# One attention and mixture-of-experts layer on one core: the expert inputs and x1 turned by transposing DMAs, with x1's rows kept as half-precision pairs

## The chip, the cores and the metric

The kernel runs on 1 core of one Trainium2 chip, in one launch. The metric is the device time of one execution, in microseconds (us). The runs of the kernel before have a median of 424.5 us (423.6 to 426.48, three runs).

## The reference

4 sequences of 1024 tokens with 128 channels go through one attention block and one mixture-of-experts block, each with a residual and a layer norm. Cut to what matters:

```python
q, k, v = silu(x @ Wq), silu(x @ Wk), x @ Wv          # 16 heads of 8
energy = einsum('bhnd,bhmd->bhnm', rope(q), rope(k)) * tril
out = einsum('bhnm,bhmd->bhnd', energy, v) * sigmoid(x @ Wg1 @ Wg2)
x1 = layernorm(x + (norm(out) * ln_w + ln_b) @ Wo)    # called x1 in the kernel
top_v, top_i = top_k(x1 @ gate_w, 2)                  # 8 experts, 2 for each token
g, u = x1 @ Wg[e], x1 @ Wu[e]                         # 128 -> 352
expert_out = sum over the 2 experts of p[e] * (silu(g) * u) @ Wd[e]
shared = (silu(x1 @ Sg) * (x1 @ Su)) @ Sd             # 176 wide, every token
y = layernorm(x1 + expert_out + shared)
```

The attention has no softmax, so the kernel computes it as a causal linear attention with a running state.

## The kernel before

The 4096 tokens are 32 tiles of 128 rows (P = 128), in 8 quads of 4 tiles (R = 4). The program for each engine is written out by hand, with semaphores between them; nothing is planned by a tool. It has four stages.

**Setup** (to 17 us) loads and splits weights.

**Attention, x1 and routing** (17 to about 196 us) run as one software pipeline: a loop over steps s = 0 to 37 on every engine, and in step s each engine works on the pieces of several tiles. Of tile t, the energies are made in step t, masked and summed in t+1, projected in t+2 (L583), and in t+3 ACT writes the normalised x1 twice (L796), as two rows of 132 f32 values in SBUF (`x1_rows`: 128 channels, the destination DEST, the gate weight). In step t+4 PE turns the row (L580, a transpose against the identity into the bank `b_p`), ACT copies the result to f16 (`x1T_hi`, L778), and DVE subtracts that from the PSUM value and so gets the low half (`x1T_lo`, L1000). In step t+5 PE multiplies both halves with the router's weights (L558 to L560). The order in a step on DVE is: masks, `x1T_lo`, routing work in some steps, `rope_add`, `add_x`, `x1_shifted`, `gate`, statistics, `rope_cos` (L920). The variance of x1 goes round four engines: ACT sums squares (L788), POOL makes `rstd` (L1280, L1282), DVE makes `x_plus` and `x_shift` (L970, L978), ACT writes x1 (L796). After each quad is ranked, POOL scatters its rows to DRAM with 8 indirect DMAs (L1288, 64 in all, each of 128 rows), one to the region of each token's first expert and one to that of its second. SP loads the inputs' transposed tiles (L416), one in each step.

**Shared expert and the end of routing** (about 180 to 237 us): the shared expert's matmuls over quads (L600 to L602, L616, L617) with DVE's `shared_add` (L1058), the table of slot tiles (DVE), and SP's 8 fill DMAs behind each expert's region.

**Routed experts** (237 to 391 us): 39 slot tiles of 256 slots, of which 35 hold real slots and the rest are dummies. They go through a ring of U = 4 buffers. For slot tile t: SP reads its address from a table (a value load), waits until PE has turned tile t-4 and DVE has copied its `slot_meta`, and loads 256 rows of 528 bytes (L442, from DRAM into `slot_rows`). PE turns them (L654, two f32 transposes into the bank `b_in`, in `slot_turn`). ACT copies the result to f16 (L861), DVE subtracts for the low half (L1174, in `evac`), and then copies DEST and WEIGHT out of the row (L1178); this last copy waits until the scatter of tile t-4 has landed (`y_scattered`). PE makes gate and up (L669 to L671, 18 matmuls of 256 columns, f16), ACT the silu (L869, three), DVE the product (L1186, three), PE the down projection in f32 (L685, 12 records, into the single bank `y_ps`), ACT the scaling by the gate weight (L880, two), and POOL scatters the result to `ydram` in DRAM (L1321, two indirect DMAs of 128 rows).

PE's order of work is fixed: up of tile t, turn of tile t+1, down of tile t-1. Up of t waits for DVE's low half of t (`slots_copied`); down of t-1 waits for `hidden_done` of t-1 and for the scaling of t-2, since there is one y bank.

**End** (to 425 us): SP reads four counts (`real_scatters`, L446), waits for the last scatters (L449), loads the results (L452, 16 DMAs of 256 KB), and PE, DVE and ACT make the last sum and layer norm, which SP stores (L460).

## Time and profile before

| | |
|---|---|
| runs, median (lowest to highest) | 424.5 us (423.6 to 426.48) |
| profiled execution, its own time | 426.87 us |
| its span in the profile | 425.0 us |
| mean granted TensorE clock | 0.959 of full |
| busy in the span: PE, PEld, DVE, ACT, POOL | 347.0, 271.8, 257.6, 235.0, 233.5 us |
| chain that ended last, by engine | PE 51%, DVE 15%, issue 11%, ACT 10% |

PE is the matmul engine and PEld its weight loads, which overlap it. The profiled execution is 1.9 us longer than its span, and 2.4 us longer than the median of the runs.

### The profile page before, as it was taken

How to read it: one execution, taken by the hardware profiler on the slowest of the kernel's cores; microseconds unless marked ns; L12 is line 12 of the kernel's file. 1: busy time of each engine (PE TensorE's matmuls, PEld its weight loads, DVE VectorE, ACT ScalarE, POOL GpSimd, SP SyncE). 2: the span in 40 equal slices, each digit the busy share in tenths (PEclk: the TensorE clock that was granted, in tenths of full speed). 3: DMA queues.
4: the chain of work that ended last, by engine and by line, in shares of the span. 5: the costliest groups of instructions: out<-in, count | busy, mean ns of one | idle time of the engine just before them, and what ended most of it. 6: DMA issues, size and time to landing. Idle time of an engine off the chain costs nothing.

```text
span 425.0 us, 12763 instructions
## 1 busy us (share of the span) xinstructions
PE 347.0 (82%) x4172; PEld 271.8 (64%) x4172; DVE 257.6 (61%) x826; ACT 235.0 (55%) x861; POOL 233.5 (55%) x302
## 2 busy tenths in 40 slices
PE   3798888787978887886489898897977979889980
PEld 2476656565756655645347797877977878779730
DVE  1469998978797879787555443333443433434682
ACT  3587779687877868523112354444454444445354
POOL 3377636768585868777640044534444345344682
PEclk9999999999899989999969999989999899899986
DMA  8956000101011110101232022212212222121784
GB/s 222 331 165 152 16 22 20 47 29 45 28 47 34 41 41 21 35 25 49 64 107 66 27 65 68 73 50 64 77 57 59 63 61 74 52 71 38 219 294 131
DMA packets 32280, 33.47 MB, mean 79 GB/s; under 512 B 4784, under 2 KB 27632, under 8 KB 32080
## 3 DMA queue, kind: packets, MB, share of 16 engines
q1 hardware_dynamic: 27360, 23.19, 18.9%
q0 software_dynamic: 4544, 9.45, 6.8%
q8 instruction: 36, 0.59, 0.6%
q14 instruction: 20, 0.16, 0.1%
q10 hardware_dynamic: 320, 0.08, 0.1%
HBM read 21.16 MB, written 13.56 MB: 82 GB/s over the span
## 4 chain that ended last, share of the span: by engine, by line
PE 51%; DVE 15%; issue 11%; ACT 10%; another core or an unknown queue 3%; POOL 3%; DMA 2%; SPq 2%; DVEq 1%; ACTq 0%; POOLq 0%
PE b_p L685 9%; PE b_es L671 6%; PE b_es L669 5%; PE b_es L670 4%; DVE masked_energies L938 4%; PE b_in L477 3%; PE b_es L502 3%; ACT turns L763 2%; PE b_es L514 2%; ACT ffn_staged L869 2%; PE b_o L534 2%; DMA x_rows<-ydram 2%; PE b_in L654 1%; PE b_o L528 1%
## 5 line engine op out<-in xcount | busy, mean ns | idle before, releaser
L1321 POOL DMA_INDIRECT ydram<-ffn_staged,slot_meta x78 | 74.9, 960 | 111.6 <-ACT ffn_staged L880 92.1
L1186 DVE TENSOR_TENSOR ffn_staged<-ffn_staged,b_es 128x256 f32<-128x256 f32 x79 | 31.8, 420 | 78.3 <-ACT ffn_staged L869 57.6
L1288 POOL DMA_INDIRECT rows<-x_rows,place x64 | 65.4, 1023 | 16.0 <-issue 13.6
L669 PE MATMUL b_es<-slots_T,w_hi 128*128 128x256 f16 x158 | 45.4, 287 | 19.2 <-DVE slots_T L1174 18.3
L685 PE MATMUL b_p<-w_down,ffn_staged 128*128 (+1 forms) x468 | 58.7, 275 | 1.0 <-issue 1.0
L685 PEld LDWEIGHTS b_p<-w_down,ffn_staged 128*128 128x128 f32 (+1 forms) x468 | 55.3, 191 | 1.2 <-issue 1.1
L869 ACT ACTIVATE ffn_staged<-b_es 128x256 f32<-128x256 f32 x79 | 29.2, 385 | 33.9 <-PE b_es L671 28.3
L763 ACT ACTIVATE turns<-b_turn,const_sb 128x128 f32<-128x128 f32 x128 | 36.5, 368 | 16.6 <-PE b_turn L488 15.9
L671 PE MATMUL b_es<-slots_T,w_lo 128*128 128x256 f16 x158 | 45.4, 287 | 0.0
L670 PE MATMUL b_es<-slots_T,w_hi 128*128 128x256 f16 x158 | 45.3, 287 | 0.0
L880 ACT ACTIVATE ffn_staged<-b_p,slot_meta 128x128 f32<-128x128 f32 x78 | 24.4, 366 | 35.9 <-PE b_p L685 34.1
L938 DVE TENSOR_TENSOR masked_energies<-b_es,const_sb 128x512 f32<-128x512 f32 x64 | 41.0, 680 | 1.8 <-PE b_es L502 1.4
L477 PE MATMUL b_in<-w_raw,xT_ring 128*128 128x384 f32 x64 | 30.6, 564 | 9.2 <-DMA ln_w_b<-in_ln 6.7
L796 ACT ACTIVATE x_rows<-x_plus,x_shift,rstd 128x256 f32<-128x256 f32 x32 | 19.2, 600 | 27.4 <-DVE x_shift L978 27.0
L1253 POOL TENSOR_TENSOR turned_qk<-qk,const_sb 128x256 f32<-128x256 f32 x32 | 26.2, 820 | 13.5 <-ACT qk L738 13.4
L669 PEld LDWEIGHTS b_es<-slots_T,w_hi 128*128 x158 | 16.0, 101 | 23.9 <-issue 21.3
L752 ACT ACTIVATE v_spread<-b_in 64x64 f32<-64x64 f32 x128 | 28.3, 221 | 1.1
L528 PEld LDWEIGHTS b_o<-turns,states 128*128 128x128 f32 x56 | 8.9, 196 | 30.9 <-DVE products L948 25.4
L1280 POOL TENSOR_TENSOR var_eps<-stat,const_sb 128x2 f32<-128x2 f32 x33 | 7.2, 219 | 36.4 <-ACT squares_out L788 36.1
L502 PE MATMUL b_es<-turns 32*64 32x128 f32 x1024 | 25.5, 286 | 1.7 <-issue 1.0
L920 DVE TENSOR_TENSOR roped<-qk,const_sb 128x256 f32<-128x256 f32 x32 | 23.0, 720 | 6.0 <-ACT qk L738 5.9
L528 PE MATMUL b_o<-turns,states 128*128 128x128 f32 x56 | 13.8, 330 | 15.2 <-DVE products L948 12.4
(213 smaller groups left out, 914.6 us busy)
## 6 DMA issues: line engine op xcount, KB each, us to landing
ffn_staged<-rows SPq DMA_DIRECT2D x39, 132.0 KB, 2.1
x_rows<-ydram SPq DMA_DIRECT2D x16, 256.0 KB, 6.8
xT_ring<-in_xT SPq DMA_DIRECT2D x32, 64.0 KB, 1.8
x_sb<-in_x SPq DMA_DIRECT2D x4, 512.0 KB, 6.1
out<-x_sb SPq DMA_DIRECT2D x8, 256.0 KB, 2.3
ffn_staged<-in_Wg SPq DMA_DIRECT2D x1, 1408.0 KB, 7.5
ffn_staged<-in_Wu SPq DMA_DIRECT2D x1, 1408.0 KB, 6.7
ydram<-ffn_staged,slot_meta POOLq DMA_INDIRECT x78
```

The lines of the kernel that those rows point to most:

```text
L477: nc.tensor.matmul(b_in[:, 0:3 * P], x_t, w_raw[:, :], start=True, stop=True).then_inc(projected, 1)
L502: mm = nc.tensor.matmul(b_es[H * h:H * h + H, g, P * c:P * c + P], keys[g], queries[g][:, 2 * h:2 * h + 2, H * c:H * c + H], start=True, s ...
L669: nc.tensor.matmul(o, w, slots_T[:, j % 2, 0, :], start=True, stop=False)
L670: nc.tensor.matmul(o, w, slots_T[:, j % 2, 1, :], start=False, stop=False)
L671: mm = nc.tensor.matmul(o, wlo, slots_T[:, j % 2, 0, :], start=False, stop=True)
L685: mm = nc.tensor.matmul(y_ps[:, b * P:(b + 1) * P], hidden_T[0:n, k % 2, c, b * P:(b + 1) * P], w_down_flat[0:n, bass.ds(e * (IC * P) + c ...
L763: nc.scalar.activation(turns[:, t % TR, j * P:(j + 1) * P], b_turn[:, P:2 * P], ACT.Copy, scale=C("spread")[:, j:j + 1])
L869: nc.scalar.activation(silu_gate[:, j % 2, c, :], up_banks[j % 2][c][:, 0:SLOTS], ACT.Silu).then_inc(expert_silu_done[c], 1)
L938: nc.vector.tensor_tensor(masked_energies[:, t % 2, 2 * r:2 * r + 2, :].rearrange("p c (b n) -> p c b n", n=H), b_es[:, 2 * r:2 * r + 2, 0 ...
L1186: ins = nc.vector.tensor_tensor(hidden_T[:, j % 2, c, :], silu_gate[:, j % 2, c, :], up_banks[j % 2][c][:, SLOTS:], ALU.mult)
L1288: nc.gpsimd.indirect_dma_start(out=rows, out_offset=bass.IndirectOffsetOnAxis(ap=place[:, t // R, c, t % R:t % R + 1], axis=0), in_=x1_row ...
L1321: nc.gpsimd.indirect_dma_start(out=ydram, out_offset=bass.IndirectOffsetOnAxis(ap=slot_meta[:, j, b, 0:1].bitcast(u32), axis=0), in_=scale ...
```

## The change

It does the following.
- A row of `x1_rows` holds x1 as 128 f16 high halves and 128 f16 low halves, in the 512 bytes where 128 f32 values stood; the f32 x1 stays in `x_sb`. ACT writes `x_sb` and the high halves in two instructions of 128x128 in place of one of 128x256; DVE makes the low halves (`rows_lo`) at the end of its step, after `rope_cos`.
- PE's transpose of x1, ACT's `x1T_hi` and DVE's `x1T_lo` are gone. SP issues a transposing DMA for each tile, SBUF to SBUF (`turn_x1`), in its loop of input loads; after every fourth tile a plain DMA copies copy 0 of the quad's rows to copy 1. POOL's scatters wait for `x1_lo_done`, and the second copy's for `rows_doubled`.
- For a slot tile, SP issues a transposing DMA from DRAM straight into `slots_T` (now 4 buffers), then waits until the scatter of tile t-4 has landed, and issues a small DMA for `slot_meta` (256 pieces of 8 bytes); the load of the next tile stands behind both. PE's `slot_turn`, ACT's `slots_hi` and DVE's `evac` are gone.
- Up of t waits for its load and for `hidden_done` of t-2. There are two y banks, and down of t-1 waits for the scaling of t-3.

```diff
 x1_rows = sb("x1_rows", [P, TILES, TOP, ROW])
+x1_halves = x1_rows[:, :, :, :].bitcast(f16)
...
 projected_out = b_p[:, 0:2 * P]
-x1T_ps = b_p[:, 2 * P:3 * P]
...
 shared_y = [b_turn[:, :], b_o[:, :]]
-slots_T_ps = b_in[:, 0:SLOTS]
-y_ps = b_p[:, 0:SLOTS]
+y_ps = [b_p[:, 0:SLOTS], b_in[:, 0:SLOTS]]
...
                 sp.dma_start(w_down_chunks[0:n, :, c, :], Wd[:, c * P:c * P + n, :].rearrange("e i h -> i e h")).then_inc(ffn_loaded, 16)
+    def turn_x1(t):
+        if not tile(t):
+            return
+        sp.wait_ge(x1_lo_done, t + 1)
+        sp.dma_start_transpose(x1T[:, :, t * P:(t + 1) * P], x1_halves[:, t, 0, 0:2 * P]).then_inc(x1T_loaded[t % R], 16)
+        if t % R == R - 1:
+            quad = x1_halves[:, t + 1 - R:t + 1, :, 0:2 * P]
+            sp.dma_start(quad[:, :, 1, :], quad[:, :, 0, :]).then_inc(rows_doubled[t // R % 2], 16)
...
             load_ffn(t // 2 - XR // 2)
+        turn_x1(t - 7)
+    for t in range(TILES - 7, TILES):
+        turn_x1(t)
...
         if exists(t - U):
-            sp.wait_ge(slots_turned, t - U + 1)
-            sp.wait_ge(meta_copied, t - U + 1)
+            sp.wait_ge(expert_up_done[IC - 1], t - U + 1)
             sp.wait_ge(table_loaded, 16)
-        sp.dma_start(slot_rows[:, j, :, :], rows[bass.ds(at, SLOTS), :].rearrange("(p b) w -> p b w", p=P)).then_inc(slots_loaded[j], 16)
+        sp.dma_start_transpose(slots_T[:, j, :, :], row_halves[bass.ds(at, SLOTS), 0:2 * P]).then_inc(slots_loaded[j], 16)
+        if exists(t - U):
+            sp.wait_ge(y_scattered[j], 32 * i)
+            sp.wait_ge(table_loaded, 16)
+        sp.dma_start(slot_meta[:, j, :, :], rows[bass.ds(at, SLOTS), DEST:DEST + 2].rearrange("(b p) w -> p b w", p=P)).then_inc(meta_loaded[j], 16)
...
             t = s - 5
+            pe.wait_ge(x1T_loaded[t % R], 16 * (t // R + 1))
...
                 last = nc.tensor.matmul(ends_ps, all_ones, first_places, start=False, stop=True)
-        if tile(s - 4):
-            pe.wait_ge(x1_done, s - 3)
-            last = nc.tensor.transpose(x1T_ps, x1_rows[:, s - 4, 0, 0:P], C("identity"))
...
             pe.wait_ge(masked[0], TILES); pe.wait_ge(masked[1], TILES); pe.wait_ge(products_masked, TILES)
-        pe.wait_ge(x1T_lo_done, R * q + R); pe.wait_ge(x1T_hi_done, R * q + R)
+        for k in range(R):
+            pe.wait_ge(x1T_loaded[k], 16 * (q + 1))
...
             shared_up(q + 2)
-    def slot_turn(i, j, lag):
-        ok, t, k, r = stage(i, j, lag)
-        if not ok:
-            return
-        pe.wait_ge(slots_loaded[k], 16 * (r + 1))
-        if exists(t - 1):
-            pe.wait_ge(slots_copied, t)
-        for b in range(2):
-            mm = nc.tensor.transpose(slots_T_ps[:, b * P:(b + 1) * P], slot_rows[:, k, b, 0:P], C("identity"))
-        mm.then_inc(slots_turned, 1)
...
         t = U * i + j
-        pe.wait_ge(slots_copied, t + 1)
+        pe.wait_ge(slots_loaded[j], 16 * (i + 1))
+        if exists(t - 2):
+            pe.wait_ge(hidden_done, t - 1)
...
                 w, wlo = w_hi_flat[:, bass.ds(at, P)], w_lo_flat[:, bass.ds(at, P)]
-                nc.tensor.matmul(o, w, slots_T[:, j % 2, 0, :], start=True, stop=False)
-                nc.tensor.matmul(o, w, slots_T[:, j % 2, 1, :], start=False, stop=False)
-                mm = nc.tensor.matmul(o, wlo, slots_T[:, j % 2, 0, :], start=False, stop=True)
+                nc.tensor.matmul(o, w, slots_T[:, j, 0, :], start=True, stop=False)
+                nc.tensor.matmul(o, w, slots_T[:, j, 1, :], start=False, stop=False)
+                mm = nc.tensor.matmul(o, wlo, slots_T[:, j, 0, :], start=False, stop=True)
...
         pe.wait_ge(hidden_done, t + 1)
-        if exists(t - 1):
-            pe.wait_ge(yscaled[(j + lag - 1) % U], i + (j + lag - 1) // U + 1)
+        if exists(t - 2):
+            pe.wait_ge(yscaled[(j + lag - 2) % U], i + (j + lag - 2) // U + 1)
...
                 n = min(P, INNER - c * P)
-                mm = nc.tensor.matmul(y_ps[:, b * P:(b + 1) * P], hidden_T[0:n, k % 2, c, b * P:(b + 1) * P],
+                mm = nc.tensor.matmul(y_ps[k % 2][:, b * P:(b + 1) * P], hidden_T[0:n, k % 2, c, b * P:(b + 1) * P],
...
     pe.wait_ge(v_done, TILES)
-    slot_turn(0, 0, 0)
...
         return a[:, FT * q:FT * q + FT, :].rearrange("p t c -> p (t c)")
-    pe.wait_ge(slots_copied, SLOT_TILES)
+    pe.wait_ge(hidden_done, SLOT_TILES)
+    pe.wait_ge(yscaled[(SLOT_TILES - 2) % U], (SLOT_TILES - 2) // U + 1)
...
         nc.scalar.activation(gate_tanh[:, t % GR, :], gate_ps, ACT.Tanh, scale=0.5).then_inc(gate_tanh_done, 1)
-    def x1T_hi(t):
-        if not tile(t):
-            return
-        nc.scalar.activation(x1T[:, 0, t * P:(t + 1) * P], x1T_ps, ACT.Copy).then_inc(x1T_hi_done, 1)
...
         act.wait_ge(x1_shift_done, t + 1)
-        both = x_plus[:, t % 2, :].unsqueeze(1).broadcast_to([P, TOP, P])
-        nc.scalar.activation(x1_rows[:, t, :, 0:P], both, ACT.Identity, scale=rstd[:, 1 - t % 2, 1:2], bias=x1_shift[:, t % 2:t % 2 + 1]).then_inc(x1_done, 1)
+        for to in (x_sb[:, t, :], x1_halves[:, t, 0, 0:P]):
+            ins = nc.scalar.activation(to, x_plus[:, t % 2, :], ACT.Identity, scale=rstd[:, 1 - t % 2, 1:2], bias=x1_shift[:, t % 2:t % 2 + 1])
+        ins.then_inc(x1_done, 1)
...
     for s in range(LAST_STEP + 1):
-        if tile(s - 2) or tile(s - 4):
+        if tile(s - 2):
...
         squares(s - 2)
-        x1T_hi(s - 4)
...
         shared(q)
-    def slots_hi(i, j, lag):
-        ok, t, k, r = stage(i, j, lag)
-        if not ok:
-            return
-        act.wait_ge(slots_turned, t + 1)
-        nc.scalar.activation(slots_T[:, k % 2, 0, :], slots_T_ps, ACT.Copy).then_inc(slots_hi_done, 1)
...
         nc.vector.bn_aggr(stat[:, 1 - t % 2, 1:3], moment_parts[:, t % 2, :]).then_inc(x1_moments, 1)
-    def x1T_lo(t):
-        if not tile(t):
-            return
-        dve.wait_ge(x1T_hi_done, t + 1)
-        nc.vector.tensor_tensor(x1T[:, 1, t * P:(t + 1) * P], x1T_ps, x1T[:, 0, t * P:(t + 1) * P], ALU.subtract).then_inc(x1T_lo_done, 1)
+    def rows_lo(t):
+        if not tile(t):
+            return
+        dve.wait_ge(x1_done, t + 1)
+        nc.vector.tensor_tensor(x1_halves[:, t, 0, P:2 * P], x_sb[:, t, :], x1_halves[:, t, 0, 0:P], ALU.subtract).then_inc(x1_lo_done, 1)
...
         dve.wait_ge(shared_y_done, q + 1); dve.wait_ge(x1_done, R * q + R)
-        nc.vector.tensor_tensor(x_sb[:, R * q:R * q + R, :], shared_y[q % 2].rearrange("p (t c) -> p t c", t=R), x1_rows[:, R * q:R * q + R, 0, 0:P],
+        nc.vector.tensor_tensor(x_sb[:, R * q:R * q + R, :], shared_y[q % 2].rearrange("p (t c) -> p t c", t=R), x_sb[:, R * q:R * q + R, :],
...
             split_lo(s - TILES)
-        if s >= 5:
-            dve.wait_ge(x1T_hi_done, min(s - 3, TILES)); dve.wait_ge(squares_summed, min(s - 1, TILES))
-        x1T_lo(s - 4)
+        if quad_ranked(s) is not None or quad_routed(s) is not None or quad_second(s) is not None:
+            dve.wait_ge(squares_summed, min(s - 1, TILES))
...
         rope_cos(s + 3)
+        rows_lo(s - 3)
...
             split_lo(q + 4)
-    def evac(i, j, lag):
-        ok, t, k, r = stage(i, j, lag)
-        if not ok:
-            return
-        dve.wait_ge(slots_hi_done, t + 1)
-        nc.vector.tensor_tensor(slots_T[:, k % 2, 1, :], slots_T_ps, slots_T[:, k % 2, 0, :], ALU.subtract).then_inc(slots_copied, 1)
-        if exists(t - U):
-            dve.wait_ge(y_scattered[k], 32 * r)
-            dve.wait_ge(yscaled[k], r)
-        nc.vector.tensor_copy(slot_meta[:, k, :, :].bitcast(i32), slot_rows[:, k, :, DEST:DEST + 2].bitcast(i32)).then_inc(meta_copied, 1)
...
     def scatter(t, c):
+        if t % R == 0 and c == 1:
+            pool.wait_ge(rows_doubled[t // R % 2], 16 * (t // R // 2 + 1))
...
             pool.wait_ge(placed, t // R + 1); pool.wait_ge(weighed, t // R + 1); pool.wait_ge(destinations_set, 1)
+            pool.wait_ge(x1_lo_done, t + R)
```

## Rows read from the trace of the kernel before

**Rows 1.** Windows: start:end, length, then busy us (instructions) of PE, PEld, DVE, ACT, POOL, clock, DMA share, GB/s.
```profile
17.00:180.00 163.00, 138.68 (x2573) 102.19 (x2580) 136.32 (x428) 124.76 (x533) 113.61 (x165) 0.98 0.19 56
180.00:237.29 57.29, 43.89 (x334) 28.65 (x314) 37.18 (x111) 14.20 (x35) 28.27 (x31) 0.94 0.21 60
237.29:388.06 150.77, 132.40 (x1142) 120.72 (x1143) 59.37 (x180) 70.11 (x212) 65.09 (x68) 0.97 0.22 61
...
277.40:280.80 3.40, 3.40 (x19) 2.43 (x17) 0.84 (x2) 0.77 (x2) 1.92 (x2) 0.51 0.28 78
```

**Rows 2.** Chain in order of time, one slot tile: start us, us, what.
```profile
256.83 1.76 another core or an unknown queue
...
259.37 0.39 ACT ffn_staged L869
```

**Rows 3.** Waits, 237 to 388: engine line, waited for, us in total, times, longest.
```profile
PE b_es L669 <- DVE slots_T L1174: 18.3, 9, 2.5
```

**Rows 4.** Timeline, two slot tiles: start us, us, engine line, operation [idle before].
```profile
302.65 0.27 PE L669 MATMUL b_es<-slots_T,w_hi 128*128 128x256 f16 x1
...
304.61 0.38 PE L654 MATMUL b_in<-const_sb,ffn_staged 128*128 128x128 f32 x2
...
304.83 1.50 PE L685 MATMUL b_p<-w_down,ffn_staged 128*128 x12
...
306.17 0.27 PE L669 MATMUL b_es<-slots_T,w_hi 128*128 128x256 f16 x1
...
306.45 0.63 ACT L880 ACTIVATE ffn_staged<-b_p,slot_meta 128x128 f32<-128x128 f32 x2 [0.98 <-PE b_p L685]
...
307.83 0.96 POOL L1321 DMA_INDIRECT ydram<-ffn_staged,slot_meta  x1 [0.75 <-issue]
...
309.10 0.96 POOL L1321 DMA_INDIRECT ydram<-ffn_staged,slot_meta  x1 [0.30 <-issue]
```

**Rows 5.** DMA queues, 310.6 to 311.0: queue, packets, MB, share.
```profile
q0 software_dynamic: 32, 0.07, 53.1%
```

**Rows 6.** SP's first four slot loads in the timeline; landing of all 39.
```profile
226.31 3.67 SPq L442 DMA_DIRECT2D ffn_staged<-rows  x4
...
DMA to landing us min/median/max: 2.0/2.1/2.9
```

**Rows 7.** Groups by line, whole span: operation xcount, busy us, mean ns, idle before.
```profile
L796 ACT ACTIVATE x_rows<-x_plus,x_shift,rstd 128x256 f32<-128x256 f32 x32 | 19.2, 600 | 27.4 <-DVE x_shift L978 27.0
L778 ACT ACTIVATE x1T<-b_p 128x128 f16<-128x128 f32 x32 | 9.3, 291 | 0.4 <-PE b_p L580 0.4
L1000 DVE TENSOR_TENSOR x1T<-b_p,x1T 128x128 f16<-128x128 f32 x32 | 9.1, 285 | 11.4 <-ACT x1T L778 10.5 <-ACT squares_out L788 0.5
L920 DVE TENSOR_TENSOR roped<-qk,const_sb 128x256 f32<-128x256 f32 x32 | 23.0, 720 | 6.0 <-ACT qk L738 5.9
```

**Rows 8.** Timeline, attention: DVE near the end of a step, PE's logits.
```profile
134.07 0.54 DVE L920 TENSOR_TENSOR roped<-qk,const_sb 128x256 f32<-128x256 f32 x1
...
139.12 0.17 PE L558 MATMUL b_p<-router_w_hi,x1T 128*128 128x8 f16 x1
```

**Rows 9.** Timeline, the last tile's x1 and its logits.
```profile
195.28 0.60 ACT L796 ACTIVATE x_rows<-x_plus,x_shift,rstd 128x256 f32<-128x256 f32 x1 [2.22 <-DVE x_shift L978]
...
198.69 0.17 PE L558 MATMUL b_p<-router_w_hi,x1T 128*128 128x8 f16 x1
```

**Rows 10.** Chain in order of time, the last real scatter.
```profile
391.20 0.95 POOL ydram L1321
...
394.26 0.79 DMA ydram<-ffn_staged,slot_meta
```

**Rows 11.** SP's value loads of line 446: count, ns min/median/max, first and last start.
```profile
L446 SPq TENSOR_LOAD <-real_scatters x4: 18/270/303, 381.2 to 383.3; - x4
```

**Rows 12.** Page, DMA issues: operation xcount, KB each, median us to landing.
```profile
x_rows<-ydram SPq DMA_DIRECT2D x16, 256.0 KB, 6.8
...
xT_ring<-in_xT SPq DMA_DIRECT2D x32, 64.0 KB, 1.8
```

## What the change does to the time

> **What bounds the kernel now.** I read the windows by stage first [rows 1]. In the experts' stage PE is busy 132.40 of 150.77 us and no other engine over half, so PE is near its limit there; in the attention stage PE (138.68 of 163.00) and DVE (136.32) share the work. Then the chain of waits, in order of time, for what PE waits on in the experts' stage. In one slot tile of four ACT waits in the middle of its silus for something that the profile can't name, 1.76 us at 256.83, and its last silu ends only at 259.76 [rows 2]. What PE waits for is then DVE's low half of the next tile: 18.3 us in 9 waits, about 2.0 each, the longest 2.5 [rows 3]. Eight of the nine are such late events, one for each pass of the ring of four. They hold up silu, and because ACT's and DVE's halves of the next tile stand behind silu and product in program order, they reach PE. In undisturbed tiles PE runs without a gap: up 302.65 to 304.61 (1.96 us), turn 0.22, down 1.34, next up at 306.17 [rows 4], so 3.52 us a tile.
>
> **The change part by part, experts.** Between 237.29 and 388.06 lie 36 ups and 35 downs.
> PE loses 36 turns of 0.22: −7.9 us. The turned halves no longer depend on ACT and DVE, so a late silu doesn't stop the next up; PE can do down of t-1 and up of t+1 before it needs the late product, 3.3 us of cover for a delay of about 2.0. The 18.3 us go, if nothing else is late. The bare sum of PE is 36 × 1.96 + 35 × 1.34 = 117.5, which is 33.3 less than now; 7.9 + 18.3 of it are named, and the rest is mostly the granted clock: in 277.40 to 280.80 it was 0.51 of full [rows 1], the lower of its two levels, 1.2 GHz, some us after PE had stood idle behind a late event, and the mean of 0.97 over the stage means 4.5 us lost. I keep a good half of it as clock loss that stays, 2.5.
>
> **What is late next.** ACT and DVE lose work and are busy 70.11 and 59.37 us even now [rows 1], so they are no bound. The new loop goes through DRAM: SP now waits for the scatter of tile t-4 between the transposing load of t and the load of t+1. From up of t to up of t+5: up, down, up, down on PE 6.60; scaling until 307.08, 0.91 after the down's end at 306.17; POOL begins 0.75 later and its second scatter 1.27 after the first (307.83, 309.10) [rows 4]. That scatter's packets run at 310.6 to 311.0, so it lands about 1.9 to 2.2 us after its start [rows 5]; the last real one of the stage took until 395.05, 3.85 after 391.20 [rows 10], and I take 2.2 with 3.85 as the upper end. On SP follow the small DMA's issue and the next value load, together the spacing of SP's loads, (3.67 − 0.34)/3 = 1.11 [rows 6]. Then L, the time of the transposing DMA. The sum is 12.84 + L for 5 tiles.
> No row shows a transposing DMA. Its lower bound is the plain load of the same rows, 2.0 to 2.1 [rows 6]; the nearest upper row is the DMA of 256 KB at 6.8, one of 16 in flight together [rows 12]. I take 3.0, near the plain load, because size and direction are the same and one is in flight at a time. With L = 3.0 a tile takes 15.8/5 = 3.17, just under PE's 3.30: slack 16.5 − 15.84 = 0.66 in five tiles. A late event holds up the scaling of the tile before, which stands behind the silus in ACT's order, by about 1.4 (its 2.0 less some 0.6 of the 0.98 that ACT stands idle before a scaling [rows 4]). The slack takes 0.66 of it, so each of 8 events costs 0.74: 5.9. The stage comes to 117.5 + 5.9 + 2.5 + 0.5 for the first and last tiles = 126.4, **−24.4 us**.
> The Trainium skill ("VectorE: DVE Perf Modes", section "The three transpose paths") speaks against the change: a 128×128 two-byte transpose takes 390 ns on TensorE and 1309 ns by the DMA crossbar. For the four blocks of a slot tile that estimate gives 5.2 us, a tile of 3.6 us, and a sum about 11 us worse. Another page ("Advanced Engine Details and Errata", section "X-Bar Transpose (TRN2)") has transposing DMAs as fast as regular ones, which gives 2.1 and a sum about 4 us better.
>
> **Attention and routing, 17 to 180.** PE loses the turn (0.11 a step). ACT loses 0.29 a step [rows 7] (`x1T_hi`), and its one write of 0.600 becomes two of 128x128; the nearest rows are twice 0.29 (`x1T_hi`) and 0.60 for both halves together, so 0.57 to 0.74, taken 0.60: it ends no later. DVE's low half, 0.285, goes from the middle of the step to its tail, after `rope_cos` [rows 7]; it stays 0.285 if left alone, and may be longer beside POOL's work, as L920 is (0.54 at 134.07, 0.72 on average) [rows 7, 8]. In the tail it delays the next step's masks. The variance's loop over ACT, POOL and DVE spans two steps, so half of it counts: +0.15 in some 12 steps without routing work; in the routing steps the wait in the middle gets shorter, −0.13 in 14. The doubling DMA (256 KB a quad) and 32 more transfers may slow SBUF accesses: +0.1 a step, bounds −0.1 and +0.35. Sum **+3**, −4 to +12. A step is 163/32 = 5.1 us.
> SP's queue: after `x1_lo_done` of a step come the transposing DMA, then the next input load, needed two steps on in the same place of PE. From 134.07 + 0.54 + 0.28 for the low half and 0.1 for the semaphore, to the logits at 139.12, are 4.1 us [rows 8]. The transposing DMA is hidden up to L = 4.1; the input load behind it (0.34 issue, 1.8 landing [rows 6, 12]) has room too. Cover gone, each us of L costs half a us in 32 steps, 16 us. POOL's waits for the low halves and the doubled rows end long before: a quad's ranks come several steps after its x1.
>
> **180 to 237.** The last tile's x1 is written at 195.88; with low half, 0.1 twice and L = 3.0 its logits begin at 199.5, against 198.69 [rows 9]. **+1**, −1 to +4.
>
> **End.** SP's four value loads (L446) ran at 381.2 to 383.3, hidden [rows 11]. They now stand behind the last tiles' `slot_meta`, which waits for tile 34's scatter. That last one lands at 395.05, and only then come 0.34 and four value loads of 0.77 less what lies in the last, 2.9: **+3.3**, 0 to +4.5.
>
> **Sum.** −24.4 + 3 + 1 + 3.3 = −17.1. The profiled execution took 426.87, so 409.8; it stood 2.4 above the median of the runs, so the median comes to 424.5 − 17.1 = **407 us**.
>
> **Rivals.**
> (A) *PE alone bounds the experts*: L near 2.1 and scatters that land in 1.9 absorb the late events. For it: the loop has 1.7 us of slack then. Against: some landings are 3.85. −33.3 + 3 + 1 + 3.3 = −26: 398 us.
> (B) *The stalls come back in the new loop*: the late scaling delays the scatter, SP and the load, by as much as before. Only the turns are gained: −7.9 + 7.3 = −0.6: 424 us. For it: the loop has only 0.66 us to give.
> (C) *Slower: the transposing DMA sets the step.* Place: PE's wait for `x1T_loaded` ahead of the logits. Price: 16 × (L − 4.1) in attention; in the experts 7.2 us for each us of L (36/5), which gives 7.2 L − 49.9 with late events and clock; L − 2 more in 180 to 237; with +3 and +3.3 the total is about 24.2 L − 111. It decides from L = 4.6: 434 us at L = 5, 458 at L = 6. For it: no row shows such a DMA, and it may well be issued as several instructions of 0.34 each on SP, so that it doesn't do in one piece what the line says. Against: the plain rows of 64 and 132 KB are at 1.8 and 2.1.
>
> **Chances.** Forecast 0.47 (its own range 400 to 417), A 0.13, B 0.17, C 0.23. Changes under 1% (4.2 us) can't be told from none. Faster by over 1%: forecast and A, 0.60; within 1%: B, 0.17; slower: C, 0.23. The range takes in A with attention at its lower bound, about 393, and at the other end B and the beginning of C, 430; outside lie most of C and little of A.
>
> **What would show it.** Experts: no PE matmul of L654, PE's waits before up near zero, a tile of 3.3 to 3.4 us, the stage near 126. SP's transposing DMA: landing 3 (right), over 4.6 (C). Attention: 163 + 3, with PE's wait ahead of the logits no longer than now; in C that wait appears in every step. End: four value loads after the last scatter's landing, the first result load about 3 us behind it. The forecast is wrong if the transposing DMA lands after 4.6 us, if SP's or the DMA queue's order adds a wait that I counted at nothing, or if DVE's tail costs more than half of 0.285 a step.

## The result, and the profile after

The changed kernel takes 430.83 us (median of 20 runs, 425.22 to 437.86) against 424.5 us for the kernel before (20 runs, 420.17 to 433.64). The ratio is 1.0134, 95% interval 1.0103 to 1.0166: 1.3% slower, where 407 us was predicted. Some executions of each kernel are slower, at a lower granted clock, and all ratios here leave them out; that keeps 13 of these 20, but of the kernel before only 2 of 13 on the chip of f1_wdown, f3_pace, f4_best and f5_bestpace, whose ratios are therefore the least sure, and f3_pace's trace is of a slow execution. The profiled execution took 429.0 us, its span 427.1.

The head of the page of the changed kernel, and its windows, cut where the first and the last up of the experts begin (columns as in [rows 1]):

```profile
span 427.1 us, 12492 instructions
...
PE 343.0 (80%) x4062; PEld 261.5 (61%) x4062; DVE 243.1 (57%) x748; ACT 223.5 (52%) x822; POOL 234.6 (55%) x302
```

```profile
17.00:180.00 163.00, 130.82 (x2352) 95.90 (x2355) 131.79 (x398) 122.59 (x509) 106.20 (x155) 0.95 0.28 75
180.00:249.00 69.00, 53.75 (x515) 35.10 (x503) 44.80 (x134) 19.86 (x57) 35.41 (x41) 0.93 0.25 65
249.00:393.20 144.20, 133.04 (x1129) 116.71 (x1130) 43.77 (x112) 58.43 (x185) 69.11 (x72) 0.99 0.31 66
393.20:427.10 33.90, 17.61 (x67) 9.54 (x66) 18.14 (x88) 14.18 (x39) 17.76 (x22) 0.83 0.62 200
```

Fewer instructions, less work on PE, DVE and ACT, and a longer span. PE did 2352 matmuls by 180 us, where it had done 2573 before [rows 1]; the turns that are gone are only some 30 of the difference, so it is behind. The marks of the two kernels (start of the event in each trace, us):

| mark | before | after | difference of the stage |
|---|---|---|---|
| start of ACT's last write of x1 | 195.3 | 206.6 | +11.3 |
| last logits | 198.7 | 210.8 | +0.8 |
| first up of the experts | 237.3 | 249.0 | −0.4 |
| last up (39 tiles) | 395.0 | 393.2 | −13.5 |
| first result load | 395.1 | 396.0 | +2.7 |
| end of the span | 425.0 | 427.1 | +1.2 |

They add up to +2.1. The experts' stage did get shorter (4.15 us from up to up before, 3.79 after), by little more than half of what was predicted; the attention steps ate most of it, and the end took 4 us more.

**Attention.** Groups by line of the changed kernel between 60 and 180 us (operation xcount | busy us, mean ns | idle before), and under them the same `x_shift` instruction in the kernel before, between 60 and 170 us:

```profile
L789 ACT ACTIVATE x_sb<-x_plus,x_shift,rstd 128x128 f32<-128x128 f32 x21 | 10.4, 493 | 18.3 <-DVE x_shift L960 18.1
L789 ACT ACTIVATE x_rows<-x_plus,x_shift,rstd 128x128 f16<-128x128 f32 x21 | 10.0, 478 | 0.0
L982 DVE TENSOR_TENSOR x_rows<-x_sb,x_rows 128x128 f16<-128x128 f32 x21 | 8.6, 412 | 0.2 <-ACT x_rows L789 0.2
L960 DVE SCALAR_TENSOR_TENSOR x_shift<-stat,rstd 128x1 f32<-128x1 f32 x20 | 8.1, 406 | 0.0
```

```profile
L978 DVE SCALAR_TENSOR_TENSOR x_shift<-stat,rstd 128x1 f32<-128x1 f32 x20 | 3.0, 149 | 0.0
```

DVE's new low half takes 0.41 us on average: in 16 of the 21 steps 0.28 to 0.29, in five 0.81. `x_shift`, one column, went from 0.15 to 0.41 on average. The timeline of one step shows why (changed kernel; start us, us, engine, line):

```profile
127.29 0.34 DVE L952 SCALAR_TENSOR_TENSOR x_plus<-b_p,rstd,x_sb 128x128 f32<-128x128 f32 x1
127.34 0.47 POOL L1235 TENSOR_TENSOR states<-states,products 128x128 f32<-128x128 f32 x1
127.55 0.96 DVE L960 SCALAR_TENSOR_TENSOR x_shift<-stat,rstd 128x1 f32<-128x1 f32 x1
127.75 0.73 POOL L1221 TENSOR_TENSOR turned_qk<-qk,const_sb 128x256 f32<-128x256 f32 x1
128.43 0.28 DVE L940 SCALAR_TENSOR_TENSOR gated_out<-gate_tanh,b_o 128x128 f32<-128x128 f32 x1
```

`x_shift` ends at 128.51, when POOL's `turned_qk` ends (128.48). It was not late in starting; it stood in DVE beside POOL's work on SBUF. It is so each time: of the 20 in this window 13 took 0.15 us, and the other seven (0.42 to 1.22 us) all end 0.02 to 0.03 us after a `turned_qk`. The Trainium skill ("Trainium Architecture — The Big Picture", section "What this means for kernel authors") says that DVE and GpSimd share one pair of SBUF ports and that it is an exclusive lock; the rows agree. In the kernel before, other instructions met POOL (L920 took 0.72 on average, [rows 7]), and no `x_shift` did. Moving one instruction changed which. It also took some away: the routing's `gap` instruction (six of them between the eleventh and the last tile's x_plus) took 0.58 us before and 0.2 us or so now.

The transposing DMA of x1 was not slow. Its 32 instructions and their landing, and the one exception, in the chain of waits between 36 and 50 us (start us, us, what):

```profile
L416 SPq DMA_TRANSPOSE x1T<-x_rows x32: 1169/1177/3365, 32.7 to 207.9; - x32
...
DMA to landing us min/median/max: 2.3/2.3/7.1
```

```profile
36.94 0.29 DVE x_rows L982
37.24 7.12 DMA x1T<-x_rows
```

A median of 2.3 us, where 4.1 were free. Only the second one, issued right behind SP's three loads of w_down, took 7.1. On SP's queue the issue itself takes 1.18 us, not 0.34.

**Experts.** Waits of the changed kernel over its span (engine line waited for: us in total, times, longest):

```profile
ACT ffn_staged L854 <- remote: 40.4, 20, 3.4
...
PEld b_es L669 <- issue: 13.2, 24, 2.0
...
PE b_es L669 <- DMA slots_T<-rows: 6.1, 10, 1.8
```

"remote" is what the profile says where it sees no releaser. In the kernel before, the same row had 14.1 us in 14 waits. ACT's waits in the middle of its silus have tripled in time; they now come in 14 of the 39 tiles, where they came in 8, and where they are densest in every other one. One of them in the timeline:

```profile
278.66 0.96 POOL L1292 DMA_INDIRECT ydram<-ffn_staged,slot_meta  x1 [2.65 <-ACT ffn_staged L865]
...
279.92 0.96 POOL L1292 DMA_INDIRECT ydram<-ffn_staged,slot_meta  x1 [0.30 <-issue]
...
280.72 0.38 ACT L854 ACTIVATE ffn_staged<-b_es 128x256 f32<-128x256 f32 x1 [0.32 <-PE b_es L671]
281.19 0.96 POOL L1292 DMA_INDIRECT ydram<-ffn_staged,slot_meta  x1 [0.30 <-issue]
282.46 0.96 POOL L1292 DMA_INDIRECT ydram<-ffn_staged,slot_meta  x1 [0.30 <-issue]
284.45 0.38 ACT L854 ACTIVATE ffn_staged<-b_turn 128x256 f32<-128x256 f32 x1 [3.35 <-remote]
284.73 0.38 ACT L854 ACTIVATE ffn_staged<-b_o 128x256 f32<-128x256 f32 x1
```

PE had issued the last matmul of that up at 281.72 and gone on to the down, but the count that the second silu waits for arrived only at 284.42, and two more behind it, three within 0.3 us. Meanwhile POOL issued four scatters back to back. Before the change the scatters came in pairs with some 2.3 us between, and only one pair in four stood close behind another.

**End.** SP, in the chain of waits: the last small DMA, the last value load, the first result load.

```profile
392.99 0.39 SPq L455
...
395.36 0.27 SPq L459
...
396.05 0.35 SPq L465
```

### The profile page after: what moved, and what is told of

Same layout as the page of the kernel before. It is cut to its first block, busy times and chain, and to the rows that moved or that the text cites. A ratio compares the mean times of both kernels' runs of the same rounds, so it can differ in the third digit from the quotient of the medians.

```text
span 427.1 us, 12492 instructions
## 1 busy us (share of the span) xinstructions
PE 343.0 (80%) x4062; PEld 261.5 (61%) x4062; DVE 243.1 (57%) x748; ACT 223.5 (52%) x822; POOL 234.6 (55%) x302
## 4 chain that ended last, share of the span: by engine, by line
PE 35%; issue 17%; DVE 17%; SPq 10%; DMA 8%; ACT 7%; another core or an unknown queue 3%; POOL 2%; DVEq 0%; ACTq 0%; POOLq 0%
DVE masked_energies L920 4%; SPq L451 4%; PE b_es L515 3%; PE b_es L527 3%; PE b_o L547 3%; PE b_in L685 3%; DMA slots_T<-rows 2%; ACT turns L762 2%; DVE roped L902 2%; PE b_in L490 2%; DMA x_rows<-ydram 2%; SPq L446 2%; DMA x1T<-x_rows 2%; SPq L455 2%
## 5 line engine op out<-in xcount | busy, mean ns | idle before, releaser
L669 PE MATMUL b_es<-slots_T,w_hi 128*128 128x256 f16 x158 | 43.9, 278 | 8.6 <-DMA slots_T<-rows 6.1
L762 ACT ACTIVATE turns<-b_turn,const_sb 128x128 f32<-128x128 f32 x128 | 36.6, 368 | 17.1 <-PE b_turn L501 16.7
L670 PE MATMUL b_es<-slots_T,w_hi 128*128 128x256 f16 x158 | 43.6, 276 | 0.4 <-issue 0.4
L671 PE MATMUL b_es<-slots_T,w_lo 128*128 128x256 f16 x158 | 43.8, 277 | 0.0
L920 DVE TENSOR_TENSOR masked_energies<-b_es,const_sb 128x512 f32<-128x512 f32 x64 | 41.2, 681 | 1.7 <-PE b_es L515 1.0
L854 ACT ACTIVATE ffn_staged<-b_es 128x256 f32<-128x256 f32 x79 | 27.0, 397 | 18.0 <-PE b_es L671 13.5
L541 PE MATMUL b_o<-turns,states 128*128 128x128 f32 x56 | 13.5, 324 | 25.3 <-DVE products L930 25.3
L1221 POOL TENSOR_TENSOR turned_qk<-qk,const_sb 128x256 f32<-128x256 f32 x32 | 25.8, 805 | 12.2 <-ACT qk L737 12.1
L685 PE MATMUL b_in<-w_down,ffn_staged 128*128 (+1 forms) x228 | 30.0, 281 | 3.1 <-DVE ffn_staged L1156 3.0
L515 PE MATMUL b_es<-turns 32*64 32x128 f32 x1024 | 29.5, 300 | 3.6 <-issue 3.5
L789 ACT ACTIVATE x_sb<-x_plus,x_shift,rstd 128x128 f32<-128x128 f32 x32 | 15.8, 493 | 31.0 <-DVE x_shift L960 30.6
L685 PEld LDWEIGHTS b_in<-w_down,ffn_staged 128*128 128x128 f32 (+1 forms) x228 | 27.4, 193 | 6.2 <-issue 6.1
L685 PE MATMUL b_p<-w_down,ffn_staged 128*128 (+1 forms) x240 | 30.2, 275 | 0.0
L685 PEld LDWEIGHTS b_p<-w_down,ffn_staged 128*128 128x128 f32 (+1 forms) x240 | 28.4, 191 | 0.3
L1156 DVE TENSOR_TENSOR ffn_staged<-ffn_staged,b_turn 128x256 f32<-128x256 f32 x19 | 8.0, 421 | 34.6 <-ACT ffn_staged L854 20.6
```

The costliest lines, as they stand in the source:

```text
L515: mm = nc.tensor.matmul(b_es[H * h:H * h + H, g, P * c:P * c + P], keys[g], queries[g][:, 2 * h:2 * h + 2, H * c:H * c + H], start=True, s ...
L669: nc.tensor.matmul(o, w, slots_T[:, j, 0, :], start=True, stop=False)
L670: nc.tensor.matmul(o, w, slots_T[:, j, 1, :], start=False, stop=False)
L671: mm = nc.tensor.matmul(o, wlo, slots_T[:, j, 0, :], start=False, stop=True)
L685: mm = nc.tensor.matmul(y_ps[k % 2][:, b * P:(b + 1) * P], hidden_T[0:n, k % 2, c, b * P:(b + 1) * P], w_down_flat[0:n, bass.ds(e * (IC * ...
L762: nc.scalar.activation(turns[:, t % TR, j * P:(j + 1) * P], b_turn[:, P:2 * P], ACT.Copy, scale=C("spread")[:, j:j + 1])
```

## The experiments

A ratio is to the kernel before on the same chip, with its 95% interval; the chips differ, so marks from the traces are used beside it. "Ups" is the mean time from up to up over 39 tiles.

| kernel | ratio | last x1 at | first up | ups | ACT's "remote" waits in silus | span |
|---|---|---|---|---|---|---|
| before | 1 | 195.3 | 237.3 | 4.15 | 14.1 | 425.0 |
| changed | 1.013 (1.010 to 1.017) | 206.6 | 249.0 | 3.79 | 40.4 | 427.1 |
| e1_meta | 0.997 (0.993 to 1.000) | 209.4 | 250.7 | 3.80 | 44.7 | 425.1 |
| e2_space | 1.063 (1.056 to 1.071) | 207.2 | 249.4 | 4.36 | 0 | 453.6 |
| e3_lopool | 0.984 (0.976 to 0.991) | 199.6 | 241.6 | 3.78 | 53.5 | 419.2 |
| e4_ffn | 1.017 (1.007 to 1.026) | 210.0 | 256.5 | 3.83 | 43.7 | 436.1 |
| f1_wdown | 1.024 (1.013 to 1.034) | 207.7 | 249.8 | 3.79 | 34.8 | 426.6 |
| f3_pace | 1.011 (0.998 to 1.024) | 209.5 | 254.7 | 3.70 | 30.0 | 432.4 |
| f4_best | 0.975 (0.966 to 0.984) | 192.9 | 236.0 | 3.69 | 36.3 | 407.0 |
| f5_bestpace | 0.988 (0.978 to 0.999) | 194.8 | 236.5 | 3.67 | 18.2 | 411.8 |
| g1_x1pe | 1.002 (0.997 to 1.007) | 211.1 | 252.9 | 3.84 | 41.9 | 432.0 |
| g3_best_x1pe | 0.978 (0.969 to 0.987) | 197.6 | 239.0 | 3.79 | 49.4 | 413.4 |
| g2_metaspace | run once | 207.9 | 249.1 | 3.85 | 1.8 | 439.3 |
| h1_half | run once | 205.8 | 251.7 | 3.28 | 0 | 404.3 |

Kernels with the same attention code (changed, e1, e2, f3, g2; h1 adds eight DMAs to it) have their last x1 at 205.8 to 209.5: differences under 4 us in that column say nothing. Much of this spread is the granted clock. Between the eleventh and the last tile's x_plus (x_plus is what DVE makes just before ACT writes x1; 21 tiles) the windows are, in this order for the kernel before, the changed one, e3_lopool and f5_bestpace:

```profile
75.66:190.45 114.79, 95.26 (x1674) 68.08 (x1655) 95.33 (x314) 81.23 (x335) 85.89 (x120) 0.97 0.12 36
80.13:201.74 121.61, 95.83 (x1653) 68.12 (x1652) 99.69 (x315) 83.81 (x335) 83.68 (x120) 0.97 0.21 56
81.36:194.67 113.31, 89.09 (x1652) 63.47 (x1632) 90.87 (x293) 84.31 (x335) 94.81 (x141) 1.00 0.23 61
75.00:189.90 114.90, 90.86 (x1631) 65.83 (x1631) 90.67 (x293) 84.42 (x336) 94.18 (x141) 0.97 0.25 68
```

The changed kernel's steps are 6.8 us longer than those of the kernel before at the same clock, 0.97 of full. The same code has 121.7 in h1 (0.97), 122.5 in g2 (0.97), 124.2 in e1 (0.95), 123.2 in e2 (0.92) and 125.5 in f3 (0.89). So the clock can hide or feign some 4 us here, but it does not explain the slower steps. Nor does it explain the 11.3 us up to the last x1: h1, whose clock from 17 us to there is 0.98 as in the kernel before (the changed kernel has 0.96), is still 10.5 us behind it.

**e1_meta: the wait for the scatter off SP's queue.**
```diff
-                    sp.wait_ge(y_scattered[j], 32 * i)
+                    sp.wait_ge(meta_copied, t - U + 1)
-                sp.dma_start(slot_meta[:, j, :, :], ...
+                sp.dma_start(meta_in[:, j, :, :], ...
+                dve.wait_ge(y_scattered[k], 32 * r)      # in copy_meta, after hidden of the tile before
+                nc.vector.tensor_copy(slot_meta[:, k, ...], meta_in[:, k, ...]).then_inc(meta_copied, 1)
```


> From the changed kernel; SP no longer waits for the scatter of tile t-4 between two slot loads: the small DMA goes to a buffer of its own, and DVE copies it into slot_meta after the hidden product of the tile before, waiting there for the scatter. Theory: the loop scatter, SP, small DMA, value load, transposing load is what keeps the experts at 3.79 us a tile (145 us from the first to the last up), so the ups come about 3.45 us apart, the stage is 10 to 13 us shorter, and the four value loads before the results are hidden again (2 to 3 us). Whole kernel 10 to 14 us less than the changed one. Rival: the late counts of PE's progress that ACT waits for (3 us in every other tile) set the pace whatever SP does; then under 3 us.

The ups stay at 3.80: the loop through the scatter did not set the pace. The gain is at the end: the first result load comes 2.4 us before the last up, in the changed kernel 2.9 us after it, and from the last up to the end of the span are 30.0 us in place of 34.0. By the ratios the kernel is some 7 us faster than the changed one, between theory and rival; the traces show only these 4 of them, and a last x1 that is 2.8 us later.

**e2_space and g2_metaspace: scatters spaced by their landing.**
```diff
+                if spaced:
+                    pool.wait_ge(y_scattered[(j - 1) % U], 32 * (n if j else n - 1))
```


> From the changed kernel; POOL waits before each tile's two result scatters until those of the tile before have landed (its loop is written out for that). Theory that PE's counts come late because four scatters run back to back: the late counts (ACT waiting 2 to 3.4 us in the middle of a silu, 39 us in all) go, though each pair starts up to 1 us later; the stage is 0 to 8 us shorter. Rival: the bunches of four are only the consequence of late counts that have another cause; then the waits stay at about 39 us and the stage is 0 to 5 us longer.

> e1_meta with the full spacing of e2_space (POOL waits until both scatters of the tile before have landed). It tells whether e2_space was slow because of SP's loop through the scatter or because of POOL. Theory: POOL alone makes a tile 1.27 + 2.3 + 0.75 = 4.3 us, so the ups stay 4.2 to 4.4 apart even with the loads off that loop, and ACT has no waits of unknown cause in its silus. Rival: ups 3.4 to 3.7 apart.

In both, ACT's waits of unknown cause in the silus are gone, but for one of 1.8 us in g2. That answers the question of cause, but both are slow. In e2_space the later scatters hold up SP, and PE waits for the slots:

```profile
POOL ydram L1294 <- DMA ydram<-ffn_staged,slot_meta: 38.8, 16, 3.6
PE b_es L669 <- DMA slots_T<-rows: 33.6, 30, 2.5
```

With the loads off that loop (g2_metaspace) the ups are 3.85 apart, not the 4.3 that I expected of POOL alone; there DVE's copy waits for the scatters instead (32.2 us in 14 waits). Of the 12.2 us that g2's span is longer than the changed kernel's, 2.2 are in the experts' stage and 8.0 behind the first result load, where the granted clock was 0.70 of full and not 0.82.

**f3_pace and f5_bestpace: weaker spacing.** POOL waits for the first scatter of the tile before only.
```diff
+                if paced:
+                    pool.wait_ge(y_first[(j - 1) % U], 16 * (n if j else n - 1))
```


> From e1_meta; POOL waits before a tile's two result scatters until the first scatter of the tile before has landed (each half has its own semaphore, the loop is written out). Theory: four scatters back to back make PE's counts late, and since in e1_meta the scatters are off the path of the loads, spacing them costs little: ACT's waits in the middle of a silu fall from 44.7 us to under 10, ups come 3.4 to 3.6 us apart in place of 3.79, and it is 6 to 12 us faster than e1_meta. Rival: POOL itself becomes the bound, at 1.27 + landing 2.1 to 2.5 + 0.75 less the first scatter's own overlap, 3.0 to 4.2 us a tile; then no faster.

> f4_best with the spacing of f3_pace. The difference to f4_best is that of f3_pace to e1_meta: 6 to 12 us less if late counts from back-to-back scatters bound the experts, none or more if POOL becomes the bound.

The waits in the silus fall by a third (f3 against e1) to a half (f5 against f4), but in f5 another 19.4 us of them stand ahead of the scalings (7.4 in f3). The ups come closer by 0.1 (f3 against e1) and 0.02 (f5 against f4), and neither kernel is faster than the one that it was made from. A miss: this spacing does not stop the late counts and costs as much as it gives.

**h1_half: one scatter for each tile.** The second 128 slots of each tile are left out of the result.
```diff
-                for b in range(2):
+                for b in range(1):
                     nc.gpsimd.indirect_dma_start(out=ydram, ...
```


> e1_meta with one result scatter for each slot tile in place of two (the second 128 slots of each tile are left out of the result; ydram is filled beforehand with copies of x by eight DMAs in the attention steps, and the waits are counted accordingly). Only the experts' stage is to be read. Theory that POOL's back-to-back scatters make PE's counts late and that these cost the stage its last 0.3 to 0.5 us a tile: ACT's waits of unknown cause in its silus fall from 44.7 us to under 5, and the ups come 3.30 to 3.40 us apart, PE's own 1.96 + 1.34, in place of 3.79. Rival: the late counts have another cause; then the waits stay over 20 us and the ups over 3.5 apart.

The ups are 3.28 apart, and PE is busy all the time. The window of the stage, and two silu sequences with a scatter in each (timeline):

```profile
251.70:376.20 124.50, 124.49 (x1129) 116.31 (x1130) 51.06 (x152) 65.45 (x186) 34.46 (x36) 1.00 0.32 61
```

```profile
301.63 0.38 ACT L860 ACTIVATE ffn_staged<-b_turn 128x256 f32<-128x256 f32 x1 [0.27 <-PE b_turn L677]
301.70 0.96 POOL L1313 DMA_INDIRECT ydram<-ffn_staged,slot_meta  x1 [2.20 <-ACT ffn_staged L871]
302.29 0.38 ACT L860 ACTIVATE ffn_staged<-b_o 128x256 f32<-128x256 f32 x1 [0.27 <-PE b_o L677]
```

So the bare PE time of the prediction is right, SP's transposing loads keep up with it (PE has no wait for them here), and all that stands between 3.28 and 3.80 goes away when POOL issues half as many scatters. It halves the number, the time and the data of the scatters at once, so it doesn't say which of these holds the counts back, nor how much of the 0.52 us a tile goes through the late counts: in g2, where they are nearly gone too, the ups are 3.85 apart.

**e3_lopool: the low halves on POOL.**
```diff
-                rows_lo(s - 3)        # DVE, end of step
+                rows_lo(s - 4)        # POOL, ahead of powers(s)
```


> From the changed kernel; the low halves of x1 are made by POOL one step later, before the variance's power, in place of DVE at the end of its step; SP's transposing DMA is issued one input load later. Theory that DVE sets the attention steps: DVE loses 0.41 us a step, and the last x1 is written 6 to 10 us earlier than 206.6. Rival: the variance's loop or the DMAs set it; then POOL's extra 0.4 us ahead of the power makes it 0 to 6 us longer.

The last x1 comes 7.0 us earlier, as the theory has it (some of it with the clock, as said above), although here PE does wait for the transposing DMA:

```profile
L416 SPq DMA_TRANSPOSE x1T<-x_rows x32: 1167/1178/1929, 36.4 to 201.0; - x32
...
  PE b_p L570: 14.9, 11
```

**f1_wdown and e4_ffn: the big loads.** f1 issues SP's three w_down loads at tiles 14, 18 and 22; e4 issues all expert weights from ACT's queue.
```diff
-                if part == 2:
-                    for c in range(IC):
+                if part in (5, 7, 9):
+                    c = (part - 5) // 2
```


> From the changed kernel; SP's three loads of w_down, which stood just ahead of the second transposing DMA of x1, are issued one at a time at the input loads of tiles 14, 18 and 22, with a semaphore of their own. Theory: that transposing DMA took 7.1 us from issue to landing because those loads were ahead of it, and this is the lag that the changed kernel has from its fifth tile on; it now takes under 4 us and the whole kernel 3 to 5 us less than the changed one. Rival: the loads only delay another transposing DMA, wherever they stand; then under 1.5 us.

> From the changed kernel; the loads of the expert weights (two of 1408 KB and the rest) are issued by ACT into its own queue in steps 0, 2 and 4 in place of SP between its input loads. Theory: the 4.6 us that the changed kernel falls behind between 40 and 47 us come from the transposing DMAs and input loads standing behind those big loads in SP's queue; 3 to 5 us of them come back, less about 1 us of ACT's issue time. Rival: the 16 DMA engines themselves are full then, whatever the queue; then under 1 us.

In f1 every transposing DMA lands in 2.3 us:

```profile
DMA to landing us min/median/max: 2.3/2.3/2.3
```

But the kernel is no faster: 1.4 us ahead of the changed one at the eleventh tile's x_plus (78.7), where e2, f3 and h1, which keep these loads, have 79.1 to 79.2, and level at the last x1 (207.7 against 206.6). Nor is e4. Its first up comes 7.5 us later than the changed kernel's: it is 3.4 behind at the last x1 and loses 4.8 more between the last logits and the first up, where the clock was 0.84 of full and not 0.91 (f3 and h1 have 0.84 there too, and lose 3.4 and 4.1). The one long DMA was real, and was not worth 3 to 5 us. It may matter with e3's edit: e3_lopool has its fifth x_plus at 52.7 us, 5.3 later than the changed kernel, and f4_best, with both edits, at 45.1. Why e3 starts so late was not tested.

**g1_x1pe: x1 turned by PE again, the rows stay pairs.**
```diff
+                    last = nc.tensor.transpose(x1T_ps, x_sb[:, s - 4, :], C("identity"))
+                x1T_hi(s - 4)         # ACT
+                x1T_lo(s - 4)         # DVE, mid step
-                sp.dma_start_transpose(x1T[...], x1_halves[:, t, 0, 0:2 * P])
```


> From the changed kernel; the turn of x1 goes back to PE, ACT and DVE as in the kernel before (from the f32 x1), while the rows stay pairs: DVE still makes the low halves of the rows at the end of its step, ACT still writes x1 twice, the slots are still turned by DMA. Theory: the pairs are what costs in the attention steps and the transposing DMA is hidden, so undoing the DMA gives nothing back and adds ACT 0.29 and DVE 0.29 us a step: last x1 written 3 to 8 us later than 206.6 in the changed kernel. Rival: the transposing DMAs and the order of SP's queue cost the 11 us; then the last x1 is back within 4 us of the kernel before (195.3).

The last x1 comes 4.5 us later than in the changed kernel (1.6 to 5.3 against all those with its attention code), not earlier. The transposing DMA of x1 costs nothing and seems a small gain; the pairs are the cost.

**f4_best and g3_best_x1pe.** f4_best joins e1, e3 and f1; g3 is the same with the turn of x1 on PE.

> The meta buffer of e1_meta, the low halves on POOL of e3_lopool and the later w_down loads of f1_wdown together. If the three gains are independent (1.7, 2.9 and 1% of the changed kernel), 0.955 to 0.965 of the kernel before; if the lag of e3_lopool at its fifth tile (5.4 us behind the changed kernel) has the cause of f1_wdown's, up to 2% more.

> f4_best with the turn of x1 on PE, ACT and DVE as in g1_x1pe; the low halves of the rows stay on POOL. The difference to f4_best is the worth of the transposing DMA of x1 by itself: theory, f4_best is 3 to 8 us faster (ACT 0.29, DVE 0.29, PE 0.11 us a step, half or less of it on the path); rival, no difference, since the variance's loop over ACT, POOL and DVE sets the step.

f4_best is 2.5% faster than the kernel before by the ratio, somewhat less than was expected of the sum; the spans of the two traces, 407.0 against 425.0, are 4.2% apart. Its last x1 comes 13.7 us earlier than in the changed kernel; g3's comes 4.7 us after f4's, and 2.8 after that of f5, which has f4's attention code. The whole times of f4 and g3 can't be told apart (their intervals overlap, on different chips).

Between the eleventh and the last tile's x_plus, where the start plays no part, the steps alone give (us, from the traces; in brackets the granted clock): before 114.8 (0.97), changed 121.6 (0.97), g1 128.6 (0.95), e3 113.3 (1.00), f4 113.6 (0.98), f5 114.9 (0.97), g3 115.9 (0.97). Low halves on DVE rather than POOL: 8.3 (changed against e3), but 6.7 at the same clock (against f5). With the turn on PE in both, the same move is worth 12.7 (g1 against g3), of which some 2.6 may be the clock (e1 against the changed kernel). PE's turn rather than the DMA: on a DVE that is full 7.1 (g1 against changed) or, at g1's clock, 4.5 (against e1); on one that is not 1.0 to 2.3 (g3 against f5 and f4), which is within what two traces of the same code differ by.

## Why the prediction was wrong

**Bound now, bare PE sum: right.** The prediction has 3.30 a tile; h1_half has 3.28. **The time L of the transposing DMA: right**, 2.3 us for x1 in the trace, where 3.0 was taken, and no wait of PE for slots in h1_half. Rival C, which had this DMA set the step, did not happen: slower came by another way, the one I had written as "if DVE's tail costs more than half of 0.285 a step": the steps got 0.32 longer (6.8 us in 21). That the chances had 0.23 for slower is no merit, since it stood there for C.

**The step that failed first: attention, +3 predicted, +11.3 measured (range −4 to +12).** Two terms were mis-sized. The low half was to "stay 0.285"; it took 0.41 on average, since it now reads SBUF and in five of 21 steps meets POOL. And I counted only the instruction that moved: `x_shift` grew by 0.26 us because the order shifted it onto POOL's work, which no term held. The two add 0.38 us to a step, where I had none more and half of 0.285 moved. That is not all net: routing instructions that now miss POOL give some 0.15 back, and by the windows above DVE is busy 4.4 us longer in 21 steps (0.21 a step) and idle 2.5 us longer (0.12). The idle time is the rest of the miss: the emptier middle of the step gave nothing back, since DVE now waits there for the variance's power (8.3 us between 60 and 180, 0.9 before between 60 and 170). e3 and f5 show the size: DVE loses 8.8 to 9.0 us of work in 21 steps, and the steps get 8.3 (e3, at full clock) or 6.7 us (f5, at the clock of the changed kernel) shorter. So DVE's work counts by three quarters or more, and not by half. Of the 11.3 us, 6.8 fall in these 21 steps; the other 4.5 are there by the eleventh tile, at a like rate for each tile, and no experiment took them apart. ACT's two writes took 0.97 and not 0.60, a term that was also wrong; f5, which keeps them, has steps as long as the kernel before at the same clock (114.9 against 114.8), so they cost little.

The +3 itself was made of the wrong thing. The two terms of the low half cancelled (12 × 0.15 against 14 × 0.13), and all that was left, 32 × 0.1, was a slower SBUF under more DMA traffic. No run isolates that term, but h1_half speaks against it: with DMAs busy 0.31 of the time in these 21 steps against 0.21 its steps take 121.7 us against 121.6, at the same clock.

**Then the experts, the larger miss: −24.4 predicted for 36 ups and 35 downs, −13.5 measured over the stage.** The step that failed is "the 18.3 us go", with 8 events at 0.74 left of them. The turns' part came, 38 × 0.22 = 8.4; some 3 us are clock (0.97 over 150.8 us before, 0.99 over 144.2 after); so of the stalls only some 2 us went. I had the late events as a delay of fixed number, eight, and asked only whether PE had cover for one. The rows had shown that ACT waits for PE's count, and I did not ask what holds the count back. It is POOL's scatters (e2, g2, h1), and 8 tiles with such a wait became 14. That a PE that runs ahead brings the scatters closer together is how I read it; no run tests it. This is rival B in its result, the stalls come back, but not by its mechanism, the loop through scatter and SP, which e1 shows not to set the pace.

**180 to 237: right**, +0.8 and −0.4 against +1. **End: right in mechanism and size**, +2.7 against +3.3, and e1 gets it back; the result loads and the last sums then took 1.2 us longer, for which I have no cause.

**SP's queue.** I had 0.34 for the issue of a transposing DMA; it is 1.18 to 1.22. The one at 7.1 us behind the weight loads was not foreseen either. Neither sets the time here. The sum by the rule that a transposing DMA is as fast as a plain one was also off: with L = 2.1 the slack of 1.56 takes the whole 1.4 of each event, which is 5.9 + 0.9 = 6.8 us better by the prediction's own terms, not 4.

The misses add up: 11.3 − 3 = 8.3 in attention, 24.4 − 13.5 = 10.9 in the experts, 1.2 at the end, less 0.6 in 180 to 237 and 0.6 in SP's part of the end, 19.2 us, from −17.1 to +2.1 in the traces. The medians are 4 us further apart than the two profiled executions.

**Open.** What in a run of scatters holds back PE's counts (number of DMAs, rows or POOL's time) was not separated, nor why where it is densest it falls in every other tile, nor how much of the pace goes through it. No order was found that keeps both scatters and loses the late counts at no cost; f4_best still has 36.3 us of them and 0.4 us a tile above PE's own time, some 15 us.

## What to carry to other kernels

Price a moved instruction together with its new neighbours: an SBUF instruction of DVE that lands beside POOL's work may wait for it (here 0.15 us became up to 1.22), and what the old place hid is not hidden in the new one. Look at the granted clock of the stretch before two traces are compared by a few us. When a wait has no named releaser, find what holds the count before counting on the wait to go; a faster engine may make its cause more frequent. A transposing DMA of 64 to 128 KB that lands in 2.3 to 3 us is worth having where two steps are free, if another engine than the bound one makes what it reads.

## What the runs showed of the hardware that I had not expected

- PE's semaphore counts can arrive some 3 us after PE has issued the work and gone on, while POOL issues indirect DMAs back to back (ACT's longest wait for one was 3.4 us); with half as many, none did.
- A transposing DMA (128x256 f16, SBUF to SBUF) occupies SP's queue for 1.18 us, and lands 2.3 us after its start; a plain one of the same queue is issued in 0.34 [rows 6]. The slots' (DRAM to SBUF, twice the size) mostly landed 2.5 to 3.0 us after their start. The Trainium skill ("VectorE: DVE Perf Modes", section "The three transpose paths") gives 1309 ns for a block, by estimate 5.2 us for the slots' four; the trace doesn't agree with that product, and is nearer the rule of another page of the Trainium skill ("Advanced Engine Details and Errata", section "X-Bar Transpose (TRN2)") that a transposing DMA is as fast as a plain one, here 2.1 us.
- ACT's write of 128x128 from SBUF took 0.49, almost that of 128x256 (0.60): by these two rows most of it doesn't depend on the width.
